# Blocks of unit-matrix turns in TensorE's gaps at three seams between stages

## The reference

```python
# layer 0
h = conv1d_causal(x, w=cond) + b
h = h + attention(rmsnorm(h))            # 16 heads, 4 kv heads, head dim 128, rope, causal
tok = rmsnorm(h)
probs = softmax(tok @ gate_w.T); topv, topi = top_k(probs, 2)
h = h + sum_e combine[:, e] * ((silu(tok @ wg[e].T) * (tok @ wu[e].T)) @ wd[e].T)   # 8 experts, 176 wide
x = x + h
# layer 1
shift1, scale1, gate1, shift2, scale2, gate2 = split(cond @ ada_w + ada_b, 6)
y = ln(x) * (1 + scale1) + shift1
y = x + gate1 * (attention(y @ qkv_w + qkv_b) @ out_w + out_b)                      # 16 heads
z = ln(y) * (1 + scale2) + shift2
y = y + gate2 * (gelu(z @ ffn_w1 + ffn_b1) @ ffn_w2 + ffn_b2)
e = argmax(softmax(y @ Wr.T + br)); y = prob[e] * (B[e] @ (A[e] @ y)) / 64
x = x + y
```

## Time and profile before

| | us |
|---|---|
| three timed runs | 682.96, 683.33, 687.75 |
| median of the three | 683.33 |
| the profiled execution, its time | 688.67 |
| its span, first to last instruction | 686.9 |
| busy in the span: PE, DVE, ACT, POOL | 613.9, 394.0, 329.3, 188.0 |

### The profile page before, as it was taken

How to read it: one execution, slowest core, us unless ns; L and a number is a source line. 1 busy time by engine, 2 the same in 40 slices (tenths; PEclk the granted TensorE clock), 3 DMA queues, 4 the chain that set the end, 5 groups by cost and what they waited for, 6 DMA issues and landing times.

```text
span 686.9 us, 13256 instructions
## 1 busy us (share of the span) xinstructions
PE 613.9 (89%) x5408; PEld 511.0 (74%) x5408; DVE 394.0 (57%) x735; ACT 329.3 (48%) x836; POOL 188.0 (27%) x194
## 2 busy tenths in 40 slices
PE   3689999999995879999959999999999998589997
PEld 2577877787774758888738788888888886368776
DVE  3678778777786546765483452442524517852463
ACT  2576667756674134433225554455444343265540
POOL 0664433244331122543042331112103003532000
PEclk9578999999996788999969999999999999789999
DMA  9440000000000353444100111102000002101013
GB/s 279 156 185 2 1 2 1 3 2 1 1 2 1 121 157 116 138 138 168 63 0 1 63 31 63 31 3 62 1 2 1 1 2 62 31 0 31 1 63 123
DMA packets 12605, 36.26 MB, mean 53 GB/s; under 512 B 2152, under 2 KB 3688, under 8 KB 11936
## 3 DMA queue, kind: packets, MB, share of 16 engines
q1 hardware_dynamic: 12304, 34.36, 15.5%
q10 hardware_dynamic: 240, 1.05, 0.6%
HBM read 34.29 MB, written 1.11 MB: 52 GB/s over the span
## 4 chain that ended last, share of the span: by engine, by line
PE 78%; ACT 8%; DVE 6%; issue 3%; DMA 2%; POOL 1%; SPq 0%; DVEq 0%; ACTq 0%
PE ps L1298 18%; PE ps L1300 17%; PE ps L1299 17%; PE ps L1413 9%; PE ps L1573 4%; PE ps L1370 2%; ACT raw_s L663 2%; PE ps L1724 2%; DMA xT<-in_x_T 2%; PE ps L1398 2%; ACT hid L621 1%; PE ps L1384 1%; ACT work L656 1%; PE ps L1561 1%; PE ps L1327 1%
## 5 line engine op out<-in xcount | busy, mean ns | idle before, releaser
L1165 DVE SCALAR_TENSOR_TENSOR strm_lo<-ps,col,strm_hi 128x512 fp32r<-128x512 f32 x32 | 24.0, 751 | 114.3 <-ACT strm_hi L779 113.2
L475 POOL TENSOR_TENSOR w_lo<-raw_w,w_hi 128x1024 fp32r<-128x1024 f32 x20 | 48.9, 2462 | 133.6 <-ACT w_hi L589 110.7
L1298 PE MATMUL ps<-act_hi,w_hi 128*128 128x512 f32 x160 | 65.4, 408 | 5.6 <-POOL act_lo L537 3.3
L1298 PE MATMUL ps<-w_hi,act_hi 128*128 128x512 f32 x160 | 66.0, 412 | 4.5 <-ACT junk L582 3.1
L1413 PE MATMUL ps<-raw_w,raw_s 128*128 128x256 f32 x256 | 63.4, 393 | 6.4 <-ACT raw_s L663 6.4
L763 ACT ACTIVATE work<-ps,col 128x512 f32<-128x512 f32 x64 | 44.2, 690 | 51.3 <-PE ps L1300 51.2
L1299 PE MATMUL ps<-act_lo,w_hi 128*128 128x512 f32 x160 | 64.2, 401 | 0.0
L1299 PE MATMUL ps<-w_lo,act_hi 128*128 128x512 f32 x160 | 64.0, 400 | 0.0
L1300 PE MATMUL ps<-act_hi,w_lo 128*128 128x512 f32 x160 | 64.0, 400 | 0.0
L1300 PE MATMUL ps<-w_hi,act_lo 128*128 128x512 f32 x160 | 63.7, 398 | 0.0
L1413 PEld LDWEIGHTS ps<-raw_w,raw_s 128*128 128x128 f32 x256 | 47.9, 197 | 15.4 <-ACT raw_s L663 9.7
(11 more groups left out here) (185 smaller groups left out, 1449.2 us busy)
## 6 DMA issues: line engine op xcount, KB each, us to landing
raw_w<-in_w_attn SPq DMA_DIRECT2D x16, 512.0 KB, 4.5
raw_s<-in_w_moe SPq DMA_DIRECT2D x11, 384.0 KB, 4.3
work<-comb_dram SPq DMA_DIRECT2D x10, 256.0 KB, 3.8
work<-comb_dram SPq DMA_DIRECT2D x18, 128.0 KB, 2.9
raw_w<-in_w_qkv SPq DMA_DIRECT2D x4, 512.0 KB, 12.6
raw_w<-in_w_o SPq DMA_DIRECT2D x1, 2048.0 KB, 7.8
raw_s<-in_w_ffn SPq DMA_DIRECT2D x8, 256.0 KB, 2.8
bd<-in_w_ada SPq DMA_DIRECT2D x1, 1536.0 KB, 6.6
```

Of the source, the lines that this page charges most:

```text
L475: G.tensor_tensor(flat(w_lo[:, slot]), raw, flat(f32(w_hi[:, slot])), ALU.subtract).then_inc(s_piece_lo, 1)
L1165: V.scalar_tensor_tensor(flat(strm_lo[:, n % SS]), ps[:, 4 + n % 2, :], c_("bv", 4 * (u // CHUNKS) + h), flat(f32(strm_hi[:, n % SS])), AL ...
L1298: mm(dst, ah, bh, start=start and i == 0, stop=False, **flags)
```

## The change

A helper `keep_warm(n, bank, at)` is added to TensorE's program: n turns of the unit matrix into itself, all to the same 128 columns of a PSUM bank that holds nothing needed at that point. It is called at nine places, which makes 15 blocks with 226 turns together. Nobody reads what they write, and no wait is added or removed. The instructions of the other engines are the same.

```diff
--- before.py
+++ after.py
@@ -1333,6 +1333,11 @@
                 pe.wait_ge(s_y_act, PAIR * BT * rounds)
                 pe.wait_ge(s_y_dve, PAIR * BT * rounds)
 
+            def keep_warm(n, bank, at=0):
+
+                for _ in range(n):
+                    nc.tensor.transpose(ps[:, bank, at:at + P], ident, ident)
+
             def turn_y(t):
 
                 conv_taken(1 if t < Y_FIRST.stop else 2)
@@ -1447,12 +1452,16 @@
                     last.then_inc(s_ada_mm, 1)
                 if s == TILES:
                     pe.wait_ge(ld_small, 48)
+                    keep_warm(26, 3)
                     for t in range(3):
                         turn_h(t)
+                    keep_warm(12, 3)
                 if s >= 1:
                     if s == 1:
                         pe.wait_ge(ld_o0, 16)
                     pv0(s - 1)
+                    if s == TILES:
+                        keep_warm(16, 3)
                     if s < TILES:
                         proj(s, (NPROJ - 1,))
                     oproj(s - 1)
@@ -1510,6 +1519,7 @@
                                             ident).then_inc(s_combT_psum, 1)
 
                 if n == 3:
+                    keep_warm(34, 0)
                     pe.wait_ge(s_combT_ready, CHUNKS)
                     moe_down(0)
                 if n >= 3:
@@ -1621,7 +1631,9 @@
 
             pe.wait_ge(s_x1_ready, 1)
             for t in range(CT):
+                keep_warm((14, 14, 6, 14)[t], 0)
                 turn_z(t)
+            keep_warm(16, 0)
             pe.wait_ge(s_x1_ready, 2)
             for u in range(U + 1):
                 if u < U:
@@ -1629,6 +1641,8 @@
                 if u == 1:
                     pe.wait_ge(s_xn1_ready, TILES)
                     pe.wait_ge(s_xT1_copied, TILES)
+                if u == U:
+                    keep_warm(22, 3)
                 if u >= 1:
                     pv1(u - 1, 0)
                     pv1(u - 1, 1)
@@ -1647,7 +1661,9 @@
                         turn_x2(0)
                     out1(u - 1, 3)
             pe.wait_ge(s_q1_copied, 12 * U)
-            turn_z2(range(CT))
+            for t in range(CT):
+                turn_z2((t,))
+                keep_warm((4, 8, 8, 18)[t], 5)
 
             def ffn_up(n):
                 m, c = FFN[n]
@@ -1677,6 +1693,7 @@
                 if n < NF:
                     ffn_up(n)
                 if n == 0:
+                    keep_warm(14, 1)
                     turn_x2(1)
                 if n == 1:
                     turn_z2((4, 5))
```

## The result

The changed kernel takes 675.37 us (median of 7 runs, 673.23 to 680.15). Beside it, on the same chip, the kernel before took 684.43 us. The medians are 9.1 us apart. The ratio on record is 0.9846, with an interval of 0.981 to 0.9881; as a share of the time before, that is 10.5 us, between 8.1 and 13.0 us, and the 9.1 us lie inside it. 673 us were predicted, with a gain of 10.9 us and a range of 668.5 to 680 us.

The account below looks back on a forecast made before the run. TensorE runs at half clock behind idle gaps at the seams; 3.2 + 2.1 + 3.2 + 2.4 = 10.9 us off 683.33 us is 672.4, with the gain rounded down 673 us; range 668.5 to 680 us.

Parts of the forecast that it names:

- The bound of 19.7 us: Six listed stretches at 1.2 GHz hold 39.4 us of TensorE work; at full clock at most about 19.7 us is won.
- The turns count: At 52.79 us the clock rose during twenty turns, so 128-column turns count as activity and can raise the clock.
- The bound of 0.141 us: Pace per turn if the stationary load did not hide at all; overruns would lose about 1.2 us over the kernel.
- first seam: Attention to experts: value products 0.9 us and first half of the output projection 2.3 us, together 3.2 us won.
- experts: First down projection: 1.9 us in its 24 matmuls and 0.2 us in three cold ones behind, together 2.1 us.
- second seam: Experts to second layer: 0.9 us in the turns of z, 2.3 us in the first projection, together 3.2 us.
- third seam: Second attention to feed-forward: 1.0 us at the value products, 1.4 us around the later turns, together 2.4 us.
- The cold stretch at 236 us stays: The cold stretch from 236.4 to 243.1 us, after the output projection, gets no block and stays.
- Some blocks fail: Rival: clock falls at one or two seams despite the blocks; gain 3 to 7 us, 676 to 680 us; chance 0.21.
- Nothing that lasts: Rival: clock kept, but each seam ends on VectorE or a DMA anyway; 681 to 684 us; chance 0.07.
- The turns do not count: Rival: clock falls as before and blocks behind run at 0.19 us a turn; 7.0 us slower, 690 us; chance 0.07.
- More than that: Rival: the unaddressed cold stretch at 236.4 us goes too, 1 to 3 us more; 669 us; chance 0.03.

Follow-up runs that it names:

- the four kernels with one seam: Kernel before plus blocks at one place each: first seam 684.55 us, experts 684.38, second seam 683.72, third seam 683.86, beside 686.88 us.
- the run with narrow products: Changed kernel with each block of n turns replaced by n // 2 plain products with 8 columns: 688.64 us beside 688.0 us, ratio 1.0035.
- the repetition: The changed kernel measured once more, unaltered, on another chip: 676.53 us, ratio 0.9843 to the kernel before.
- the last experiment: Changed kernel plus five further blocks, and three turns behind every second group of conditioning products: 678.88 us, ratio 0.9885.

## Why the prediction was right, point by point

*The clock is the lever.* Right. In each of the four kernels with one seam the clock held at that seam's blocks and each was faster. In the run with narrow products, with the same places filled, the clock fell in the first two seams and the gain didn't come; at the value products of the third, where it held, they took 2.02 us as with the turns. The list of cold stretches was not complete, though: the trace of the kernel before is also at half clock near 42 to 45 us, 49 to 55 us, 328.5 to 331.9 us and 652.5 to 656 us. The bound of 19.7 us is one for the six listed.

*The turns count.* Right, but drawn from one stretch, the rise of the clock behind 52.79 us, which alone can't part the turns from what ran before them. In the profile after, the four seams are at 1.00 with the blocks in them. The Trainium skill says the opposite in "TensorE: Matmul & The Clock Gate", section "Part 4: PE-mode transpose": that transposes leave the fast clock disengaged. The trace does not agree here: by that rule the kernel would have been slower than before, near 690 us by the prediction's sum and some 687 us by the 2.4 us of the narrow products, and it took 675.37 us.

*0.109 us a turn, and all blocks fit.* Right. 34 turns take 3.87 us and 14 take 1.69 us, the last of them 0.27 us long: 3.60 us by 33 and 1.42 us by 13, 0.109 us each. All blocks ended before their gaps did, but for the second block of 14 and the block of 4, which left no idle time and delayed nothing. The bound of 0.141 us and its 1.2 us of overrun did not come.

*The sum.* By the table of starts, less what chance gave ahead of each:

| | predicted | pair of traces | alone on the chip |
|---|---|---|---|
| first seam | 3.2 | 3.2 | 2.7 |
| experts | 2.1 | 2.1 | 2.0 |
| second seam | 3.2 | 3.0 | 2.9 |
| third seam | 2.4 | 2.4 | 3.2 |
| sum | 10.9 | 10.7 | 10.8 |

The first seam is 4.83 us at the turns of `oproj` (227.30 and 222.47 us) less the 1.66 us from the start. Of it the value products gave 0.9, the projection 2.3 us, term by term as predicted. The experts' part is the step from 4.53 to 6.59 us, 1.8 us in the down projection and 0.2 us in the cold matmuls behind it, for 1.9 and 0.2 predicted. The second seam's is 0.80 us up to the projection and 2.24 us in it, for 0.9 and 2.3 predicted. The third seam's is 0.93 us up to `ffn_up(0)` and 1.48 us up to `ffn_down` (609.28 and 595.53 us), for 1.0 and 1.4; between `ffn_up(0)` and the turns behind it nothing is won, as predicted. The single runs agree with each term, but at about 2 us to either side they can't check it to tenths; the traces do that. VectorE's stall of 1.27 us is gone, and 0.46 and 0.68 us of idle time stand ahead of TensorE's turns there instead: TensorE waits for VectorE now.

*The cold stretch at 236 us stays.* Right, and it took 0.3 us of the gain: the lead falls from 4.83 to 4.53 us, because the stretch now lies more under the first up projection (5.1 us of it, 234.42 to 239.55 us, for 4.0 before, 239.20 to 243.17 us).

*The rivals.* "Some blocks fail" did not happen at the places that were counted on: in both profiled executions of the changed kernel the clock is whole beside all 15 blocks. In the repetition it fell for 3.5 us at 595.8 us, which is `ffn_down`, behind the last block and behind the gap that the change made longer; the prediction did not see that gap grow. "Nothing that lasts" is excluded by the table. "The turns do not count" had the right sign for blocks that don't hold the clock and too high a price: its 7.0 us counted each overrun in full and took the clock to fall at every place, and 2.4 us were measured. (Its term of 4.2 us in the second seam is 4.0 us by its own numbers, 50 turns at 0.08 us more.) "More than that" had its price too high: with blocks of its own the stretch at 236 us can go, and 0.3 to 0.5 us are won by it, not 1 to 3 us.

*The base.* The kernel before was put at 683.33 us and measured at 684.43 us beside the change, and of the 10.3 us that were taken off it the medians show 9.1 us: that is why 673 us became 675.37 us, near the upper end of the forecast's own 670 to 675.5 us. The ratio fits the 10.9 us better than the medians do, and neither is known to better than some 2 us, so how close they come is in part luck; that the mechanism is right rests on the traces. The guess that executions differ by how long they are cold is borne out: of seven executions of the changed kernel the two with mean granted clocks of 0.982 and 0.980 have spans of 671.6 and 671.4 us, and the one with 0.965 has 678.4 us.

## What to carry to other kernels

Where a stretch at half clock begins behind a gap of TensorE and the engine is on the path behind it, fill the gap with matmuls that nobody reads; price the gain by the same instructions at full clock elsewhere in the trace, count only what is followed by TensorE-bound work, and size the block by its pace so that it ends before what it stands beside. Half-filled gaps gave most of the gain and doubled blocks lost all of it and 3.3 us more, so err on the short side. A cold stretch whose work is followed by a wait for another engine is hardly worth a block: of two such that were tried one gave 0.3 to 0.5 us and the other nothing. And look at the new profile for gaps that grew because TensorE arrives sooner: the one ahead of `ffn_down` has no block yet.

## What the runs showed of the hardware that was not expected

- A TensorE that is busy for 13.40 of 13.40 us can be at half clock throughout. The 8-column products in two seams and the 32-column conditioning products, 6.80 of 6.80 us at 48.6 us, stood at 0.50. It isn't always so: in other executions the clock stayed at 1.00 through the conditioning products (48.6 to 55.4 us above), and at 1.00 behind the 22 instructions of 8 columns at 572.19 us.
- The same gap in front of the same instructions (1.73 us at 328 and 321 us) is followed by the lower level in one execution and not in another. The same holds for the conditioning products, and for the 1.55 us ahead of `ffn_down`, where six of nine traces fell; at 1.02 us none of four did. That is a part of the spread between executions of one kernel, and in this pair of traces it made 3.2 of 13.7 us.
- In the last experiment TensorE waited up to 0.99 us in the middle of a projection with nothing named as the cause.
